# Joining the loading stage of a fused four-layer kernel to its first attention

## What is computed

```python
x = x + _L0_xattn_ref(_layernorm(x, axis=-1), ctx_1024, ctx_1024, mask, mask, mask, Wq, Wk, Wv, Wo)
...
# 16 heads of 64: queries from the normalised x times the mask, keys and values from ctx_1024 times the mask,
# softmax over the 64 keys of the same sequence, masked keys left out, heads joined by Wo
```

## Time and profile before

| what | value |
|---|---|
| median of three executions | 1712.88 us (1707.56 to 1715.41) |
| profiled execution: span from its first to its last instruction | 1643.5 us |
| its own device time | not recorded apart from the three above |
| PE, DVE, ACT, POOL busy over the span | 81%, 62%, 57%, 36% |
| mean granted TensorE clock | 0.927 of full |

### The profile page before, as it was taken

The page is one execution under the profiler, slowest core; times in us unless marked ns, Lnnn a source line. Parts: engine busy times, 40 slices in busy tenths (PEclk is TensorE's granted clock), DMA queues, the critical chain, the costliest instruction groups (busy, mean ns, idle before and its releaser), DMA issues. The chain is left out here.

```text
span 1643.5 us, 43000 instructions
## 1 busy us (share of the span) xinstructions
PE 1333.4 (81%) x16797; PEld 1113.8 (68%) x16821; DVE 1026.8 (62%) x2574; ACT 942.8 (57%) x2144; POOL 586.4 (36%) x588
## 2 busy tenths in 40 slices
PE   4699999986899998899258975777782888888994
PEld 4588777864688888687225653676671567677994
DVE  5677777774543333789788996633335678853445
ACT  3466555642354444798635642655555889834884
POOL 2233333321000000343147860477772004444662
PEclk9799999998999999999569997899996999978997
DMA  9200000009997000231000001011113001002335
GB/s 317 59 19 19 19 19 19 2 3 135 156 181 70 1 1 1 86 118 58 0 17 18 18 5 52 28 49 49 48 50 126 15 15 41 29 31 56 93 92 175
DMA packets 143529, 94.11 MB, mean 57 GB/s; under 512 B 55776, under 2 KB 130273, under 8 KB 142817
## 3 DMA queue, kind: packets, MB, share of 16 engines
q1 hardware_dynamic: 134368, 72.86, 20.5%
q0 software_dynamic: 8960, 18.50, 3.5%
HBM read 51.20 MB, written 40.12 MB: 56 GB/s over the span
## 5 line engine op out<-in xcount | busy, mean ns | idle before, releaser
L400 POOL TENSOR_TENSOR wide_probs<-wide_probs,wide_key_mask 128x512 f32<-128x512 f32 x64 | 82.8, 1314 | 188.1 <-ACT wide_probs L521 188.1
L1536 POOL DMA_INDIRECT moe_x_rows<-moe_rows,moe_source x72 | 79.6, 1106 | 76.0 <-DVE moe_source L1632 54.4
L739 POOL MEMSET attn_v_bd<- 128x576 f32 x2 | 1.2, 617 | 268.8 <-POOLq L163 268.8
L2228 DVE TENSOR_TENSOR moe_hidden<-banks,moe_gate 128x256 f32<-128x256 f32 x104 | 43.6, 423 | 84.2 <-ACT moe_gate L2427 83.0
L769 POOL TENSOR_TENSOR attn_col_bd<-attn_col_t,group_mask_sb 128x1024 f32<-128x1024 f32 x32 | 60.7, 1897 | 97.0 <-ACT attn_row_t L966 97.0
L3045 ACT ACTIVATE moe_router<-banks,moe_rb_sb 128x512 f32<-128x512 f32 x64 | 41.4, 688 | 91.8 <-PE banks L3149 67.8
L2062 POOL DMA_INDIRECT moe_results<-moe_y_rows,moe_x_rows x72 | 68.9, 958 | 51.8 <-issue 30.1
L1890 POOL DMA_INDIRECT moe_rows<-moe_xhat,moe_slot x64 | 61.9, 967 | 69.1 <-DVE moe_slot L2190 50.1
L843 DVE TENSOR_REDUCE attn_top<-banks 128x32 f32<-128x2048 f32 x32 | 73.1, 2283 | 18.6 <-PE banks L1027 18.6
L995 ACT ACTIVATE attn_probs<-attn_probs 128x1024 f32<-128x1024 f32 x64 | 65.9, 1053 | 27.9 <-DVE attn_probs L872 26.4
L1542 POOL DMA_INDIRECT moe_results<-moe_y_rows,moe_dest x72 | 73.0, 1014 | 22.4 <-issue 20.7
(11 more groups left out here) (434 smaller groups left out, 4313.4 us busy)
## 6 DMA issues: line engine op xcount, KB each, us to landing
moe_rows<-route_empty_sb SPq DMA_DIRECT2D x8, 2624.0 KB, 22.6
attn_ctx<-in_ctx_t SPq DMA_DIRECT2D x48, 128.0 KB, 2.1
moe_x_rows<-moe_rows SPq DMA_DIRECT2D x72, 66.0 KB, 1.9
moe_pack_sb<-in_moe_pack SPq DMA_DIRECT2D x8, 578.0 KB, 3.9
moe_w_sb<-in_moe_w SPq DMA_DIRECT2D x2, 2048.0 KB, 10.1
moe_hot<-moe_results SPq DMA_DIRECT2D x16, 256.0 KB, 6.0
moe_until_back<-moe_results SPq DMA_DIRECT2D x16, 256.0 KB, 5.7
moe_pack_sb<-in_moe_pack SPq DMA_DIRECT2D x9, 384.0 KB, 4.2
```

What stands on the lines that cost most here:

```text
L400: nc.gpsimd.tensor_tensor(probs[b.parity][:, :, h2], probs[b.parity][:, :, h2], keys, ALU.mult).then_inc(masked, 1)
L1536: nc.gpsimd.indirect_dma_start(x_rows[s % GATHERS][:], None, rows, bass.IndirectOffsetOnAxis(ap=source[:, s:s + 1], axis=0)).then_inc(gath ...
```

## The change

The loading block is gone. Its transfers and its DVE work are put into the streams of `wide_attention`. `x` comes in pieces of 4, 12, 8 and 8 tiles. The group `wide` is split in three (`wide_q` with the mask column, `wide_k`, `wide_v`), each awaited where it is first used. The scale of the first four tiles is taken by itself at the start, that of tiles 4 to 15 at step 3, that of the second half at step 12. The query weights are split before the key weights. The 56 later transfers are sent three per step from step 8 on.

```diff
-QUARTERS = 4
...
-                for q in range(QUARTERS):
-                    if q == QUARTERS // 2:
-                        start_loads(core, sp, names[:2])
...
-            start_loads(core, sp, names[2:])
...
-            for q in range(QUARTERS // 2):
-                ins = quarter_stats(core, dve, q)
-            ins.then_inc(core.first_stats, 1)
-            dve.wait_ge(core.first_stats, 1)
-            norm_scale(core, dve, FIRST_HALF)
+X_PIECES = [slice(0, 4), slice(4, HALF_TILES), slice(HALF_TILES, 24), slice(24, TILES)]
+
+def load_x(core, sp, n):
+    part = X_PIECES[n]
+    sp.dma_start(core.x[:, part], ...).then_inc(core.loaded_x[n], DMA_INC)
+
+def first_stats(core, dve, n):
+    dve.wait_ge(core.loaded_x[n], DMA_INC)
+    for t in range(X_PIECES[n].start, X_PIECES[n].stop):
...
+    ins.then_inc(core.first_stats, 1)

# sync
-                    if s.i is None and s.off == 3:
-                        start_loads(core, sp, later)
+                    if s.off < LATER_FROM:          # LATER_FROM, LATER_EACH = 8, 3
+                        between(s.off)
+                    else:
+                        for group, name in later_loads[(s.off - LATER_FROM) * LATER_EACH:(s.off - LATER_FROM + 1) * LATER_EACH]:
+                            sp.dma_start(w[name][:], args[name]).then_inc(core.loaded[group], DMA_INC)
+                def between(step):
+                    if step == 0:
+                        load_x(core, sp, 1)
+                    if step == 2:
+                        start_loads(core, sp, ["wide_v"])
+                    if step == 4:
+                        start_loads(core, sp, ["wide_later"])
+                        load_x(core, sp, 2)
+                    if step == 6:
+                        load_x(core, sp, 3)
+                load_x(core, sp, 0)
+                start_loads(core, sp, ["ident", "wide_q", "wide_k"])

# gpsimd, scalar: query weights before key weights, wait for each group apart
-                arrived(core, act, "wide")
+                arrived(core, act, "wide_q")
+                nc.scalar.copy(wq_high[:], w["wide_wq"][:]).then_inc(split_high, 1)
+                arrived(core, act, "wide_k")
                 nc.scalar.copy(wk_high[:], w["wide_wk"][:]).then_inc(split_high, 1)
-                nc.scalar.copy(wq_high[:], w["wide_wq"][:]).then_inc(split_high, 1)

# vector
+                first_stats(core, dve, 0)
+                dve.wait_ge(core.first_stats, 1)
+                norm_scale(core, dve, X_PIECES[0])
+                arrived(core, dve, "wide_q")
+                queries(0, X_PIECES[0])
...
-                    if s.i is None and s.off == 2:
-                        quarter_stats(core, dve, 2)
-                    if s.i is None and s.off == 3:
-                        quarter_stats(core, dve, 3).then_inc(core.first_stats, 1)
+                    if s.off == 2:
+                        first_stats(core, dve, 1)
+                    if s.off == 3:
                         dve.wait_ge(core.first_stats, 2)
-                    if s.i is None and s.off == 4:
+                        norm_scale(core, dve, X_PIECES[1])
+                        queries(1, X_PIECES[1])
+                    if s.off == 8:
+                        first_stats(core, dve, 2)
+                    if s.off == 10:
+                        first_stats(core, dve, 3)
+                    if s.off == 12:
+                        dve.wait_ge(core.first_stats, 4)
                         norm_scale(core, dve, SECOND_HALF)
-                        queries(1, SECOND_HALF)
+                        queries(2, SECOND_HALF)

# tensor
-                arrived(core, pe, "ident", "wide")
-                pe.wait_ge(split_low, 2)
+                arrived(core, pe, "ident")
+                            if p.off == 0 and n == 0:
+                                pe.wait_ge(split_low, 1)      # before the first query projection, 2 before the first key projection
```

More of the change, by code:

```diff
@@ L143, in __init__ @@
         self.first_stats = self.sem("first_stats")
+        self.loaded_x = [self.sem(f"loaded_x{n}") for n in range(len(X_PIECES))]
         self.newton, self.norm_links = self.sem("norm_newton"), 0
@@ L258, in arrived @@
         eng.wait_ge(core.loaded[group], core.loads[group])
[L261 to L296 removed]
+X_PIECES = [slice(0, 4), slice(4, HALF_TILES), slice(HALF_TILES, 24), slice(24, TILES)]
+def load_x(core, sp, n):
+    part = X_PIECES[n]
+    sp.dma_start(core.x[:, part], core.args["x"].rearrange("(t p) c -> p t c", p=P)[:, part]).then_inc(core.loaded_x[n], DMA_INC)
+def first_stats(core, dve, n):
+    dve.wait_ge(core.loaded_x[n], DMA_INC)
+    for t in range(X_PIECES[n].start, X_PIECES[n].stop):
+        ins = core.nc.vector.bn_stats(core.stats[:, t], core.x[:, t])
+    ins.then_inc(core.first_stats, 1)
 def halved_step(s):
@@ L348, in wide_attention @@
         LAG = 6
+        LATER_FROM, LATER_EACH = 8, 3
+        later_loads = [(group, name) for group in later for name, _, _ in GROUPS[group]]
+        assert len(later_loads) <= (TILES + LAG - LATER_FROM) * LATER_EACH
         def stages(s):
@@ L409, in _ @@
             def _(dve):
-                arrived(core, dve, "wide")
                 def queries(n, tiles):
@@ L486, in body @@
                     p, b, c, e, d = stages(s)
-                    if s.i is None and s.off == 7:
+                    if s.off == X_PIECES[1].start:
                         act.wait_ge(query_ready, 4)
+                    if s.off == HALF_TILES:
+                        act.wait_ge(query_ready, 6)
                     if s.off % 2 == 0 and s.inside(TILES):
@@ L562, in body @@
                     if e.inside(TILES):
+                        if e.off == 0:
+                            arrived(core, pe, "wide_v")
                         pe.wait_ge(normed, e.at(1, 1))
@@ L607, in body @@
                             at = 4 * (p.off % 2) + 2 * n
+                            if p.off == 0 and n == 0:
+                                pe.wait_ge(split_low, 2)
                             project(p_bank[n], (at, at + 1), wk_high, wk_low, ctx_high, ctx_low, k_made)
```

31 lines of the change are left out of this document (6 added, 25 removed).

## The result

| | time, us | against the kernel before |
|---|---|---|
| kernel before, 20 executions | 1715.39 (1705.22 to 1733.44) | |
| changed kernel, 20 executions | 1709.55 (1700.99 to 1715.84) | 0.9967, 95% interval 0.9951 to 0.9983 |
| forecast | 1696.2 (1688 to 1705) | 0.990 |

The kernel became faster by 0.33%, or 5.7 us (2.9 to 8.4), where 16.7 were forecast: by the 0.5% of the prediction it is no change. The direction was right, the size was not, and two of the mechanisms were missed: how often DVE and POOL hold each other up, and a halt of PE at step 8. Another 2.5 us of the distance to the 1696.2 are no error of mechanism: the forecast started from 1712.9 us, the median of three executions, and the twenty have 1715.4.

A forecast was written before the change was run, and what follows sets the result against it. PE's idle time before about 65 us, waiting on the start, DVE's key copies and the third context pair, and its lower clock. -9.9+2.7-4.8-5.4+0.7 = -16.7 us from 1712.9 gives 1696.2 us, range 1688 to 1705.

The forecast's parts named there:

- the scaled queries (0.4): At the start on DVE, after four statistics and the chain: making the scaled queries takes 0.4 us, ending at 8.95.
- The start: First query projection on PE at 11.55 us instead of 21.44, since only the first piece of `x` is awaited: -9.9 us.
- rival (b): POOL holds up operations of DVE's chain, two at step 12 and one at step 3: +3.3, so 1699.5 us; chance 0.11.
- Steps 2 and 3: More statistics in step 2 (+0.4), chain and queries ahead of the low part of `x` in step 3 (+2.3): +2.7 us.
- Step 4: DVE loses the chain and queries there, so PE's wait of 7.75 us is cut to about 3: -4.8 us.
- the case of -15.1: PE works at its lower clock after both remaining halts, in steps 3 and 4; step 3 costs 1.6 us more.
- The third pair: The third context pair arrives by 15 us, so PE's idle 5.39 us before the values at 60.65 goes: -5.4 us.
- Steps 8 to 12: Statistics of steps 8 and 10 fit DVE's idle time, transfer issues cost nothing, chain and queries in step 12 cost +0.7 us.
- The check at step 32: Step 12's working tried on the kernel before: DVE has 4.83 us more, PE stands 2.45 where it gives 1.5.
- Rival (a): PE's clock stays up at 2.4 GHz through the first steps: -20.4, 1692.5 us; chance 0.16.
- (c): DVE holds step 5 in the third pair's place and half the start's gain is lost: -6.4, 1706.5 us; chance 0.09.
- Rival (d): TensorE stays at 1.2 GHz in steps 1 to 8, 7 us per step; 1724 us at four more; chance 0.03.

The follow-up runs named there:

- the two cut kernels: The kernel before and the changed kernel, both ended after the first attention and then storing `x`: 389.69 us and 382.68 us.
- cut_dve_splits: The changed kernel cut after the first attention, with both splits of the weights on DVE behind the first scaled queries, no longer on POOL: 377.38 us.
- cut_later_at_3: The changed kernel cut after the first attention, with the 56 later transfers back in one piece at step 3, ahead of the third context pair: 389.58 us.
- cut_after: The changed kernel ended after the first attention, the other seven parts left out: 382.68 us.

## Why the prediction was wrong

The signs of its terms were right: both halts it named shrank or went, and the new one in step 3 came with its size (3.53 against about 3.5). What failed first is the step "the scaled queries (0.4)". More widely, DVE's short operations were priced as if POOL stood still. By the leads of the two cut kernels the missing 9.4 of 16.7 us are in these terms:

- **The start**, -9.9 forecast. Measured -6.4 (15.30 against 21.66 in the second profile of the kernel before) or -8.7 (13.16 against 21.82 in the cut kernels). The failed step is "the scaled queries (0.4)": they took 2.4 to 4.6 us. I had rival (b), the chain held by POOL, and placed it at steps 3 and 12; it struck where POOL's longest operations are, because the change set them beside the queries, which before had run at 12.43 with POOL idle until 14.88. The working itself had both times, POOL's first split from 7.2 us and the end of the chain at 8.55, and did not set them side by side. With that step mended the sum comes out (11.50 in `cut_dve_splits`), though there two smaller errors cancel.
- **Steps 2 and 3**, +2.7: +3.6. The chain and the queries in step 3 cost 2.6 (2.3 forecast), 0.5 of it one operation that POOL held (as at 24.64 above). Another 0.8 to 0.9 lie in step 1, where the first key products ran 0.21 us apart throughout, and before the change only the first two of them.
- **Step 4**, -4.8: -2.4. 1.8 of the missing 2.4 are PE's lower clock in step 3: behind its halt of 3.4 to 3.5 us its products stand 0.21 us apart where 0.12 is the rule (granted clock 0.50, the level of 1.2 GHz), and DVE waits for the keys. The prediction had priced this, at 1.6, and left it to the case of -15.1; the row is below. A further 1.1 us is against "from the maxima to the end of the key copies nothing changes": POOL's key mask now ran at the same time as DVE's sum and product, which `cut_later_at_3` confirms. 0.7 came back, since the scores of step 5 ran faster (1.33 us, 1.99 before).
- **The third pair**, -5.4: -5.6. Right, and by its mechanism, in three comparisons (5.6 here, 5.9 alone, 6.9 in time when taken back).
- **Steps 8 to 12**, +0.7: +2.0 by the maxima of step 9, 1.8 of it at step 8, and +2.4 from there to step 13, nearly all the chain's. The first was costed at "nothing" for SP; I asked only whether the context pairs come in time and not what else uses the DMA engines. For the second the sum had 0.7. What it left out is POOL: 0.56 us on the first operation of the chain and 1.1 on the two of the division, 1.7 together. The check at step 32 had the same in it. There the working gave 1.5 and PE stood 2.45, and the division was held for 1.0 us behind the stretch in which I looked for such meetings; the row is below.
- **Steps 13 to 32**, 0: +1.3, in small halts of 0.3 to 0.7 us that both kernels have at varying steps. What sets them stays open.

The stretch in step 3 of `cut_after` (columns as in the earlier trace rows), and DVE's division at step 32 of the kernel before:

```profile
28.00:32.00 4.00, 4.00 (x21) 4.00 (x21) 2.07 (x5) 2.08 (x4) 0.21 (x1) 0.50 0.00 0
340.97 1.95 DVE L456 TENSOR_TENSOR wide_probs<-wide_probs,wide_inverse 128x1024 f32<-128x1024 f32 x1
```

The terms sum to -7.3 with the start at -8.7, and 7.0 are timed. Of the signs, the new halt of step 3, the free start of step 5 and the third pair's early issue (10.1 us) held; the first projection (15.30), the halt before step 5 (4.27), that of step 12 (2.18 where below 2 was said) and the lead of 15 to 20 us from step 6 on (13) did not. Rival (a) was wrong, (b) was the nearest in mechanism, (c) in size by chance. Rival (d) did not occur; its price of 7 us a step should be near 8 by its own ratio. The range of 1688 to 1705 was too narrow, since the holds were given to one rival at +3.3 and not to each place where POOL and DVE meet: at the start, in step 3, in step 4, in step 12.

## What to carry to other kernels

When a change puts work of DVE and of GpSimd side by side that used to follow each other, write both engines' times next to each other and price each short operation on DVE at what is left of the GpSimd operation beside it, first of all the ones a chain waits for; and look for the longest. A later DVE can also slide into a GpSimd operation that it used to miss, as in steps 4 and 12. Moving a long chain within a full step only changed who waits for it, while cutting the one of step 12 in two removed its halt. The large transfers for later stages cost 1.9 us until they were sent in pieces, even where there was time enough for them. Small gains should be measured on a kernel cut behind the stage in question, where executions spread over 1.6 us and not 28, and then be claimed for that stage alone.

## What the runs showed of the hardware

- An operation of DVE on 128x4 elements with two inputs took 2.32 us beside a GpSimd product of 2.34 us, and 0.16 beside none. One with a single input tensor (a scalar product on 128x12) took 0.74 us beside a GpSimd operation of 0.73, where 0.17 is the rule. Not every operation is held: the reciprocal between two held ones kept its 0.25 us (39.11 in the changed kernel, GpSimd at work from 37.77 to 40.27). Which of them is caught differs between executions of the same kernel.
- PE stood 1.25 us between two products of one group while 2 MB transfers filled the DMA engines (share 0.88 in that stretch), and did not with the same bytes in pieces of up to 256 KB, which also spread them over more steps.
- PE's lower level followed even short halts: after 3.44 us its granted clock was 0.50 over the next 4 us. In the kernel before it stood 2.46 us and had 0.58 in the stretch from 342 to 344; after the halt of 2.18 us at step 12 of the changed kernel it stayed at 1.00.
- The same kernel took about 1718 us in some sets of executions and about 1645 in others. Up to 1000 us their profiles differ by 1 to 3 us; the 64 us lie in the sparse parts.
